# Row maxima of an attention turned as 32 columns by one transpose and put into q by small transfers

## What is computed

```python
x = L0_attn_x                                   # 4 x 512 x 512
xn = _layernorm(x, axis=-1)
# attention: q, k of 8 heads x 8 channels from one projection, v from another
scores = jnp.einsum('bhqd,bhkd->bhqk', q, k)    # 4 x 8 x 512 x 512
attn = jax.nn.softmax(scores, axis=-1) / 8.0
out = jnp.einsum('bhsl,bhlv->bhsv', attn, v)
attn_out = out.reshape(b, n, 64) @ Wo_w.T + Wo_b
# experts
_, top_idx = jax.lax.top_k(xn @ W_gate + b_gate, 2)
y_all = jax.nn.relu(jnp.einsum('bsd,edh->bseh', xn, W_e) + b_e)
y = jnp.take_along_axis(y_all, top_idx[..., None], axis=2).mean(axis=2)
return x + attn_out + y
```

## Time and profile before

| | us |
|---|---|
| median of 3 runs | 293.84 |
| lowest, highest | 293.02, 297.24 |
| the profiled execution | 295.66 |
| its span on the core, first to last instruction | 293.9 |
| PE busy in the span | 281.8 |
| DVE, ACT, POOL busy | 212.5, 167.6, 192.1 |

### The profile page before, as it was taken

How to read it: one execution, slowest core, us unless ns; L and a number is a source line. 1 busy time by engine, 2 the same in 40 slices (tenths; PEclk the granted TensorE clock), 3 DMA queues, 4 the chain that set the end, 5 groups by cost and what they waited for, 6 DMA issues and landing times.

```text
span 293.9 us, 5495 instructions
## 1 busy us (share of the span) xinstructions
PE 281.8 (96%) x1710; PEld 187.2 (64%) x1710; DVE 212.5 (72%) x432; ACT 167.6 (57%) x254; POOL 192.1 (65%) x221
## 2 busy tenths in 40 slices
PE   7999999989999999999999999999999999999994
PEld 2688995848877777777777778776333333333342
DVE  3998898846876678676767786666778897885234
ACT  2669982964433333333433333345999788879961
POOL 4259979763776676699668766435657888888400
PEclk9799999778999999999999999999999999999999
DMA  7999799670554454434445455511699999999933
GB/s 233 391 400 381 256 314 404 236 277 36 168 167 144 151 162 142 157 109 158 142 141 163 118 178 148 141 49 60 194 308 295 159 231 182 148 226 196 180 105 145
DMA packets 27559, 57.27 MB, mean 195 GB/s; under 512 B 3079, under 2 KB 3208, under 8 KB 27404
## 3 DMA queue, kind: packets, MB, share of 16 engines
q1 hardware_dynamic: 19264, 37.49, 35.6%
q0 software_dynamic: 7728, 18.62, 30.3%
q10 hardware_dynamic: 540, 0.80, 0.8%
HBM read 38.29 MB, written 18.61 MB: 194 GB/s over the span
## 4 chain that ended last, share of the span: by engine, by line
PE 79%; DVE 11%; DMA 3%; issue 3%; ACT 2%; POOL 0%; SPq 0%; POOLq 0%; ACTq 0%; DVEq 0%
PE ps_l L1373 37%; PE ps_o L1291 8%; PE ps_l L1260 7%; PE ps_l L1351 7%; PE ps_l L1187 5%; PE ps_r L1212 3%; PE ps_r L1236 3%; DMA row_in<-xn_rows,gather_i 2%; PE ps_l L1335 2%; DVE row_max L1015 2%; PE ps_r L1224 2%; DMA row_in<-in_L_attn_x_dram 1%; DVE t_lo L882 1%; PE ps_l L1171 1%; ACT probs L781 1%
## 5 line engine op out<-in xcount | busy, mean ns | idle before, releaser
L1373 PE MATMUL ps_l<-w_split,t_hi 128*128 x312 | 101.3, 406 | 0.7 <-issue 0.7
L603 POOL TENSOR_TENSOR row_mid<-row_mid,bias_o 128x512 f32<-128x512 f32 x39 | 51.7, 1325 | 43.7 <-ACT row_mid L747 43.7
L1015 DVE TENSOR_REDUCE row_max<-ps_r 128x1 f32<-128x512 f32 x112 | 73.1, 683 | 9.9 <-PE ps_r L1236 7.0
L747 ACT ACTIVATE row_mid<-row_mid 128x512 f32<-128x512 f32 x39 | 24.7, 633 | 85.3 <-DVE row_mid L1038 82.7
L781 ACT ACTIVATE probs<-ps_l 128x1024 f32<-128x1024 f32 (+1 forms) x63 | 62.2, 1016 | 10.9 <-PE ps_l L1260 8.1
L1373 PEld LDWEIGHTS ps_l<-w_split,t_hi 128*128 128x128 f32 x312 | 56.6, 191 | 11.3 <-issue 1.2
L1373 PE MATMUL ps_l<-w_split,t_lo 128*128 x156 | 61.9, 397 | 0.0
L637 POOL DMA_INDIRECT acc<-expert_rows,slots_i x32 | 49.7, 1553 | 15.4 <-issue 8.7
L1038 DVE TENSOR_TENSOR row_mid<-ps_l,bias_e 128x512 f32<-128x512 f32 x39 | 27.0, 692 | 33.9 <-PE ps_l L1373 33.9
L579 POOL DMA_INDIRECT row_in<-xn_rows,gather_i x39 | 38.1, 976 | 8.3 <-issue 3.4
L1373 PEld LDWEIGHTS ps_l<-w_split,t_lo 128*128 128x128 f32 x156 | 29.6, 190 | 6.8
(11 more groups left out here) (210 smaller groups left out, 424.3 us busy)
## 6 DMA issues: line engine op xcount, KB each, us to landing
expert_rows<-row_mid SPq DMA_DIRECT2D x39, 256.0 KB, 2.0
xn_rows<-row_mid SPq DMA_DIRECT2D x16, 256.0 KB, 5.3
w_split<-in_L_ffn_W_e_dram SPq DMA_DIRECT2D x8, 512.0 KB, 5.7
w_split<-in_L_ffn_W_e_dram SPq DMA_DIRECT2D x4, 1024.0 KB, 11.2
acc<-in_L_attn_x_dram SPq DMA_DIRECT2D x16, 256.0 KB, 5.1
out_dram<-res SPq DMA_DIRECT2D x16, 256.0 KB
row_in<-in_L_attn_x_dram SPq DMA_DIRECT2D x8, 256.0 KB, 5.7
w_split<-in_L_attn_x_dram SPq DMA_DIRECT2D x8, 256.0 KB, 6.8
```

The costliest lines, as they stand in the source:

```text
L603: pool.tensor_tensor(row_mid[:, n % 4, :], row_mid[:, n % 4, :], bias_o[:], ALU.add).then_inc(y_done, 1)
L1015: dve.tensor_reduce(row_max[:, b % 2, h, i:i + 1], ring_bank(item), AX.X, ALU.max).then_inc(freed_by_dve, 1)
L1373: mm = pe.matmul(ps_y[:, n % 2, :], a[:, n % 2, ks], rhs, start=(k == 0), stop=(k == 3 * KC - 1))
```

## The change

PE now turns only the maxima. DVE writes them into a tile of their own, `max_cols`, 32 columns for each g (two parts x 4 query tiles x 4 heads). One transpose makes 32 rows of 128 of them in the bank, ACT copies 32x128 into `max_rows`, and SP's queue moves them into `q_t` by 8 transfers for each (b, g), each of 4 rows of 512 bytes, from four neighbouring partitions to partitions s, s + 32, s + 64 and s + 96. The logits wait for the transfers' semaphore `max_moved` in place of ACT's copy. The jobs stay in their places on PE. POOL's two layouts wait for the first turn of q, which alone reads `lay` now. The constants `before`, `ramp` and `lower` share their memory with `max_rows`, and the two semaphores of the added expert rows (`ya_in`, `yb_in`) are one, `y_added`, waited at 16 and at 32.

The core of the diff:

```diff
+        max_rows = sb("max_rows", [2 * QT * HG, G, P], F32R)
+        max_cols = sb("max_cols", [P, G, 2, QT, HG], F32)
...
+        def wait_moved(eng, b, g):
+
+            eng.wait_ge(max_moved, 16 * 2 * QT * (G * b + g + 1))
...
+            def move_max(b, g):
+
+                if (b, g) != (0, 0):
+                    sp.wait_ge(max_moved, 16 * 2 * QT * (G * b + g))
+                wait_kept(sp, ("max", b, g))
+                for s in range(2):
+                    for i in range(QT):
+                        rows = slice((s * QT + i) * HG, (s * QT + i + 1) * HG)
+                        sp.dma_start(q_t[b][s:P:32, g, i * P:(i + 1) * P].bitcast(F32), max_rows[rows, g, :].bitcast(F32)).then_inc(max_moved, 16)
+
+            MOVES_AT = {15: (0, 0), 23: (0, 1), 31: (1, 0)}
             for n in range(NS):
                 sp.wait_ge(y_done, n + 1)
                 sp.dma_start(y_dram[n * P:(n + 1) * P, :], row_mid[:, n % 4, :]).then_inc(y_out[n % 4], 16)
+                if n in MOVES_AT:
+                    move_max(*MOVES_AT[n])
...
+            MOVES_BEHIND = {0: ((1, 1), (2, 0)), QT: ((2, 1),), QT + 2: ((3, 0),), 2 * QT: ((3, 1),)}
             for i in range(NT):
+                for b, g in MOVES_BEHIND.get(i, ()):
+                    move_max(b, g)
                 store(i)
...
                 if n == 26:
-                    wait_filled(pool, ("max", 0, 1))
+                    wait_filled(pool, ("q", 0, 1))
                     lay_out(pool, pool_step, steps, 2, "q")
...
-            wait_filled(pool, ("max", 1, 1))
+            wait_filled(pool, ("q", 1, 1))
             lay_out(pool, pool_step, steps, 3, "q")
...
-                elif kind in ("q", "max"):
+                elif kind == "q":
                     dst = q_t[b][:, g, :]
+                elif kind == "max":
+                    if b >= 1:
+                        wait_moved(act, b - 1, g)
+                    act.activation(max_rows[:, g, :], ring_bank(job)[0:2 * QT * HG, 0:P], ACT.Copy).then_inc(freed_by_act, 1)
+                    return
...
-                dve.wait_ge(q_laid[b], 1)
+                if b >= 1:
+                    wait_filled(dve, ("max", b - 1, g))
...
-                link(dve.tensor_scalar(heads[:, :, :, 0].bitcast(F32R), mx, -1.0, None, ALU.mult))
-                dve.scalar_tensor_tensor(out=heads[:, :, :, 1], in0=mx, scalar=-1.0, in1=heads[:, :, :, 0],
+                link(dve.tensor_scalar(max_cols[:, g, 0].bitcast(F32R), mx, -1.0, None, ALU.mult))
+                dve.scalar_tensor_tensor(out=max_cols[:, g, 1], in0=mx, scalar=-1.0, in1=max_cols[:, g, 0],
...
+                if kind == "max":
+                    pe.wait_ge(max_laid, 2 * b + g + 1)
+                    mm = pe.transpose(bank[0:2 * QT * HG, 0:P], max_cols[:, g].rearrange("p s i j -> p (s i j)"), ident[:])
...
                 if kt == 0 and half == 0:
-                    wait_kept(pe, ("max", b, g))
+                    wait_moved(pe, b, g)
```

More of the change, by code:

```diff
@@ L72, in attention_and_experts @@
         ident = sb("ident", [P, P], F32)
-        before = sb("before", [P, P], BF16)
         ones = sb("ones", [P, P], BF16)
-        ramp = sb("ramp", [P, P], F32)
-        lower = sb("lower", [P, NE, NE], F32)
+        const_era = ExitStack()
+        before = sb("before", [P, P], BF16, const_era)
+        ramp = sb("ramp", [P, P], F32, const_era)
+        lower = sb("lower", [P, NE, NE], F32, const_era)
+        const_era.close()
+        max_rows = sb("max_rows", [2 * QT * HG, G, P], F32R)
         eps_t = sb("eps_t", [P, 1], F32)
@@ L96, in attention_and_experts @@
         v_second_0 = sb("v_second_0", [P, QT, HG, 2 * VC], F32)
-        sb("chosen_gap", [P, 2 * NT * 8 + 4 * 6 + NT * 2 + 8 * NT - (1 + QT) * HG * 2 * VC], F32)
+        max_cols = sb("max_cols", [P, G, 2, QT, HG], F32)
+        sb("chosen_gap", [P, 2 * NT * 8 + 4 * 6 + NT * 2 + 8 * NT - (1 + QT) * HG * 2 * VC - 2 * H * QT], F32)
         row_max = sb("row_max", [P, 2, H, QT], F32)
@@ L229, in attention_and_experts @@
         max_laid = sem("max_laid")
+        max_moved = sem("max_moved")
         logits_ready = sem("logits_ready")
@@ L236, in attention_and_experts @@
         acc_in = [sem(f"acc_in{i}") for i in range(NT)]
-        ya_in = [sem(f"ya_in{i}") for i in range(NT)]
-        yb_in = [sem(f"yb_in{i}") for i in range(NT)]
+        y_added = [sem(f"y_added{i}") for i in range(NT)]
         y_relu = sem("y_relu")
@@ L632, in _, with add_rows @@
                 pool.wait_ge(y_out[s], 16 * ((NS - s + 3) // 4))
-            def add_rows(i, r, before_it, landed):
-                pool.wait_ge(before_it[i], 16)
+            def add_rows(i, r):
+                if r == 0:
+                    pool.wait_ge(acc_in[i], 16)
+                else:
+                    pool.wait_ge(y_added[i], 16)
                 pool.indirect_dma_start(acc[:, i, :], None, y_dram,
                                         bass.IndirectOffsetOnAxis(ap=slots_i[:, r, i:i + 1], axis=0),
-                                        compute_op=ALU.add).then_inc(landed[i], 16)
+                                        compute_op=ALU.add).then_inc(y_added[i], 16)
             for i in range(NT + 2):
@@ L644, in _ @@
                 if i < NT:
-                    add_rows(i, 0, acc_in, ya_in)
+                    add_rows(i, 0)
                 if i >= 2:
-                    add_rows(i - 2, 1, ya_in, yb_in)
+                    add_rows(i - 2, 1)
         @block.scalar
@@ L1091, in result @@
                 job = ("out", b, i)
-                dve.wait_ge(yb_in[n], 16)
+                dve.wait_ge(y_added[n], 32)
                 if n >= 4:
@@ L1202, in fill @@
                 bank = ring_bank(job)
-                if kind in ("k", "q", "max"):
-                    if kind == "k":
-                        pe.wait_ge(k_laid[b], 1)
-                    elif kind == "q":
-                        pe.wait_ge(q_laid[b], 1)
-                    else:
-                        pe.wait_ge(max_laid, 2 * b + g + 1)
+                if kind == "max":
+                    pe.wait_ge(max_laid, 2 * b + g + 1)
+                    mm = pe.transpose(bank[0:2 * QT * HG, 0:P], max_cols[:, g].rearrange("p s i j -> p (s i j)"), ident[:])
+                elif kind in ("k", "q"):
+                    pe.wait_ge(k_laid[b] if kind == "k" else q_laid[b], 1)
                     src = lay[(K_LAY if kind == "k" else Q_LAY)[b]]
@@ L1240, in first_logits @@
                 rows = slice(32 * job[2], 32 * job[2] + 32)
-                wait_kept(pe, ("max", 0, 0))
+                wait_moved(pe, 0, 0)
                 wait_bank(pe, job)
@@ L1296, in last_rows @@
             def last_rows(part):
-                pe.wait_ge(yb_in[NT - 1], 16)
+                pe.wait_ge(y_added[NT - 1], 32)
                 pe.wait_ge(exp_done, 2 * LAST - 1)
```

1 line of the change is left out of this document (removed).

## The result

| us | before | after |
|---|---|---|
| median of the runs timed side by side | 294.16 (4 runs) | 300.35 (4 runs) |
| the profiled execution | 295.66 | 299.82 |
| its span | 293.9 | 298.1 |
| PE busy in the span | 281.8 | 278.8 |

The ratio is 1.0215, with an interval from 1.0173 to 1.0256: the changed kernel is 6.2 us slower, outside my range (291.8 to 298.0). Over 2% slower had 8% of mine; the interval lies on both sides of 2%. Timed again in a later batch it took 305.09 us, ratio 1.0364 (1.0301 to 1.0426). Its eight executions lie between 299.8 and 306.7 us, where the kernel before has 293.0 to 297.2. Kernels in which PE waits for moves in unit 24 or 28 ran at scattered speeds; the comparisons leave out executions over 1.5% above a kernel's fastest, so I give the spread with the medians.

What follows compares the result with a forecast made beforehand. PE was taken to bound the tile loop and the attention units; - 2.4 us for the turns + 1.8 + 0.2 of waits = - 0.4 us, from the median 293.84 to 293.4 us, range 291.8 to 298.0 (8 in 10).

Steps and rivals of the forecast that it cites:

- 7 p + L: Time from a group's first move issue on SP's queue to its last landing: seven issue intervals plus one landing, 2.94 + 2.2 us.
- PE bounds both stages: PE sets the time in tile loop (busy 20.00 of 20 us) and attention units (9.68 of 10).
- A turn costs 0.33 us less: Each of eight turns of maxima on PE, one instruction for four, saves 0.33 us; 2.4 us taken for all.
- p = 0.42 us: Time from one move's issue to the next on SP's queue, taken near SP's stores; ends 0.28 and 0.77.
- L = 2.2 us: Time from a group's last move issue to its landing, taken near a store's 2.0; ends 2.0 and 5.1.
- The wait in unit 28, 1.8 us: PE needs group (3,1) at 273.26 but its last move lands at 275.1, so PE stands for 1.8 us.
- Unit 24, 0.2 us in place of a margin of 0.8: Group (3,0) lands at 263.2, 0.8 us before its use at 264.03; 0.2 us put for pieces behind a store.
- (1,1) has room: Behind 16 loads of acc; last load there at 225.3, user at 231.67; slipping 6 us would make PE wait at unit 12.
- (2,1) has room: Turned at 242.82 and needed at 252.55: 9.7 us against ACT's copy, some 1.3, and 5.1 us for the moves.
- The clock: Rival: unit 28's wait brings PE's half clock back for 4 us, losing 2 us: 295.4 or 299 us; 4%.
- The third rival: Each move waits for a whole add on its DMA engine, eight moves taking 11.9 us: 305.8 us; 4%.
- The second rival: Slow small transfers: late moves cost 4.2 us in unit 28 and 1.6 in unit 24: 297.2 us; 18%.

Runs made afterwards that it cites:

- e4: The changed kernel without each token's second expert row, so 16 of the 32 indirect adds are left out: 305.24 us, a single execution.
- e6: The changed kernel with (3,0) turned in unit 20 and (3,1) turned with q, the old way, in unit 25, 56 moves left: 293.46 us, ratio 0.9997 to before.
- e12: The changed kernel itself, unchanged, timed again in a later batch: 305.09 us, 11 us over the kernel before.
- e1: The changed kernel with batch 3's two groups of maxima turned and copied the old way, 48 of 64 moves left: 293.35 us, ratio 0.9978 to before.
- e5: The changed kernel, all 64 moves, with (3,0) turned in unit 20 and moved behind the fourth store, (3,1) turned in unit 25: 298.45 us, ratio 1.0068.
- e11: The changed kernel with unread matmuls ahead of the waits in units 24 and 28, timed beside the changed kernel: 298.86 us, ratio 1.0182 to before.
- e2: The changed kernel with unread matmuls on PE, 8 ahead of unit 24 and 15 ahead of unit 28: 299.29 us, ratio 1.0205 to before.
- e3: The changed kernel with only the high part of the maxima moved, four transfers a group in place of eight: 295.48 us, ratio 1.0047 to before.
- e8: The kernel before, without moves, with PE made to wait in unit 28 for tile 13's second added row: 299.11 us, ratio 1.0167.
- e9: The changed kernel with only the tile loop's three groups moved, the last stage's five turned the old way: 292.87 us, ratio 0.9948 to before.
- e10: The changed kernel with (1,1) moved behind the eighth load of acc, (3,0) turned in unit 20, (3,1) the old way: 292.68 us, ratio 0.9936 to before.

## Why the prediction was wrong

The time of the moves was mis-sized (7 p + L, items 3 and 4), so the waits in units 28 and 24 came to 3.63 and 2.07 us where the sum had 1.8 and 0.2, and the clock behind them, 1.5 to 6 us, was in no term. Step by step:

1. *PE bounds both stages.* Right, and the direction of every effect followed from it.
2. *A turn costs 0.33 us less; I took 2.4 for eight.* Right for the single turn, wrong as a sum. The tile loop: the first turn of the maxima and the one in unit 2 stood at 116.60 and 207.44 before and stand at 114.20 and 204.29 after, so the three groups of the tile loop gained 0.75 us in the profiled pair (0.67 to 0.77 in all twelve profiled executions with the change), where I had 1.0. Among the units 0, 0, 0.4, about 0.3 and about 0.3: the first two went into waits for banks; the last two I read from the turn to the next unit's values or to the user of the group. Some 1.75 us in all, not 2.4. The failed part is the step from "PE is busy 9.68 of 10 us" to "what PE saves comes off": two of five turns stand in a round of scores, maximum and next scores that DVE and PE pass through in turn.
3. *p = 0.42 us.* Wrong; an issue is 0.497 us, with 0.54 from one to the next, and an occasional one of 0.96. It lies between my ends, 0.28 and 0.77, but I took the value near SP's stores. It is the same with and without adds (e4). On (3,1) it cost 3.81 - 2.94 = 0.9 us.
4. *L = 2.2 us.* Wrong; 2.94 to 4.52 us beside the adds, 1.53 without them. I had set 7 p + L for both late groups; (3,1) was short by 0.9 + 0.7 us, and (3,0) by 4.30 - 2.94 = 1.4 and 3.63 - 2.2 = 1.4.
5. *The wait in unit 28, 1.8 us.* 3.63. The chain turn, copy, first issue was right (1.49 us against 1.37), as was PE's arrival (4.75 us behind the turn against 4.71); the difference is p and L.
6. *Unit 24, 0.2 us in place of a margin of 0.8.* 2.07. This is the largest miss of a term taken singly: a margin of 0.8 us against ends that were 3 us apart (p = 0.77 or L = 5.1 would have eaten it) was near no margin. It was also drawn up as 0.33 us too wide: I let PE come to unit 28 earlier by the shorter turn, but not to unit 24. From turn to user it was 8.33 us before and, without the wait, 8.05 after.
7. *(1,1) has room, and would make PE wait if it slipped by 6 us.* It slipped by some 6.7: I had the last load's landing at 16.8 us from the first load's issue, and the moves behind it landed at 23.5. PE waited 0.4 us in unit 12 of after, 1.5 in e6, 1.1 in e4 and nothing in e12. That second bound was well placed. *(2,1) has room*, in the same paragraph, was wrong by the same p and L: in e12 its last move landed 9.7 us behind the turn (1.35 to the first issue, 3.81 for seven more, 4.52 to land), where PE came after 9.4. PE waited for it 0.4 us in e12, 0.2 in e1 and 1.0 in e5.
8. *The clock*, named as a rival at 4% and in none of the sums. The waits alone make the kernel slower, 4.7 and 5.5 us in e11 and e2, where the clock stays up. The clock adds 1.5 us in one execution (1.0 in unit 28 and 0.5 behind it) and 6.0 in the other (1.3 + 4.7). I had a row with a half clock for 4 us, forecast a wait of PE in its busiest stage, and still treated the two as independent.
9. *The third rival, each move behind a whole add on its engine*, 11.9 us for eight moves. It fell in size: 7.9 us from the first issue to the landing, of which 4.3 are issue. Its direction held, since a move lands in 1.53 us when the adds are gone and in 2.9 to 4.5 beside them. The rule of the Trainium skill that I weighed there (DMA: Bandwidth & Descriptors, "Queues, rings and completion order"), engines that go round their queues packet by packet, agrees with a landing that the adds stretch, but not with a whole add ahead of every move.

The sum with measured terms, from the first load of `acc` on: - 1.0 for the turns, + 0.4 + 2.1 + 3.6 of waits, + 1.5 of clock = + 6.6, of 7.3 measured (92.69 - 85.38); 0.3 of what is left stands behind unit 24's wait, where the clock was low too. The measured 7.3 less the 0.75 of the tile loop are + 6.6, beside 6.2 in the medians.

The second rival ("slow small transfers") had 5.8 us of waits, 18% and 297.2 us. The waits it had in units 24 and 28 came to 5.7, and that it was so near is luck: it had p = 0.77 and L = 2.2 where 0.54 and 2.9 to 3.6 were measured, too much of the one and too little of the other. What it lacked was the clock, and that the gain was less. Nothing in my cases had both a wait over 3 us and a clock that answers it, except "299 with the slow one's" in a half sentence.

**Left open.** What decides whether the clock falls, and whether it stays low for 3 us or 14. Waits of 3.63 and 3.77 us were followed by 3 and 14 us of half clock, waits of 2.1 us by 3 (unit 24 of after and of e12), 14 (e3) and 17 (e4), one of 2.8 by about 7 (e8). One of 1.1 for DVE was followed by 3 (e4), those of 1.1 and 1.2 in e5, of 1.1 for a move in e4 and of 1.5 in e6 by none. It doesn't go by the length of the wait alone. Also open is how much the layout of the shared memory, made in the same change, does: no run has it alone. The two profiled executions with the old layout (before, e8) come to the first turn of the maxima at 116.6 and 117.3 us, with a granted clock of 0.60 and 0.50 between 64 and 68 us; the twelve with the new one come to it at 114.2 to 115.5, with 1.00 there. The profiled execution before is also 1.8 us above its median, so this may be layout or chance, and it can hold a part of what e9 and e10 gain. And one move per group in place of eight wasn't tried.

## What to carry to other kernels

Each of these small transfers held its queue for half a microsecond, more than a store of 256 KB: replace work on the bounding engine by n transfers only where n issues, and a landing taken from where the DMA engines are full, fit between producer and user with room to spare. Where PE is near 100% busy, price a wait of a microsecond or more on it with the clock that may fall behind it, here up to 6 us more, and look for it in each execution rather than in one profile. Before counting a saving on the bounding engine, look what its next instruction waits for: two of five savings ended at a bank that DVE still had to read.

## What the runs showed of the hardware

- A transfer of 4 rows of 512 bytes within the core's memory holds SP's queue for 497 ns, with 0.54 us from one to the next; a store of 128 rows of 2 KB from the same queue takes 332: here the transfer with fewer bytes took longer to issue. It landed in 1.53 us at a DMA share of 0.01 (e4) and in 2.9 to 4.5 beside indirect adds, at shares of 0.7 to 1.1.
- TensorE's granted clock fell to 0.50, 1.2 GHz, within 2 us behind every wait of 2.1 to 3.8 us in which PE idled, and behind some of about 1 us, in a stage in which it is otherwise busy, and it stayed there while PE was busy 4.00 of 4 us, for 3 to 17 us. Matmuls that nobody reads kept it at the upper level through a wait of the same length.
- Of eight moves issued behind 16 loads of 256 KB, the last landed 11 to 14 us after its issue (after, e4 and e6).
- A maximum of 128x512 on DVE took 0.7 us, and PE's next scores into a bank that it frees started 0.05 us behind its end.
